# A paced row gather: 105 of 128 gathers on the GpSimd queue each wait for a point of TensorE's work

## The reference

```python
x = x + tanh(g_xattn[0]) * _L0_xattn_ref(_layernorm(x), ctx, ctx, ...)   # 16 heads, window of 32
x = x + tanh(g_ffn[0])   * _L0_ffn_ref(_layernorm(x), ...)               # 64 experts, 8 per token, and a shared one
x = x + tanh(g_xattn[1]) * _L1_xattn_ref(_layernorm(x), ctx, ctx, ...)   # 16 heads
x = x + tanh(g_ffn[1])   * _L1_ffn_ref(_layernorm(x), ...)               # 8 experts, 2 per token
```

## Time and profile before

| | us |
|---|---|
| median of three runs | 1473.32 (1467.35 to 1481.7) |
| the profiled execution | 1459.74 |
| its span, first to last instruction | 1457.9 |
| PE busy, share of the span | 1101.0, 76% |
| POOL busy, share of the span | 694.7, 48% |
| gathers L1846 into the first half's buffers: 128, mean 961 ns | 123.0 |

### The profile page before, as it was taken

The page is one execution under the profiler, slowest core; times in us unless marked ns, Lnnn a source line. Parts: engine busy times, 40 slices in busy tenths (PEclk is TensorE's granted clock), DMA queues, the critical chain, the costliest instruction groups (busy, mean ns, idle before and its releaser), DMA issues.

```text
span 1457.9 us, 28552 instructions
## 1 busy us (share of the span) xinstructions
PE 1101.0 (76%) x9014; PEld 939.3 (64%) x9014; DVE 754.7 (52%) x2773; ACT 608.3 (42%) x1505; POOL 694.7 (48%) x767
## 2 busy tenths in 40 slices
PE   4887877775778779955676771688889986789992
PEld 3666665554567768955676671467677765779992
DVE  5586666654556557724343440555666653334363
ACT  3665444432223335523333331454544452546561
POOL 1135555556556650052443437465555466554542
PEclk9998887767879889977888885576755575779996
DMA  7434114211126556643454443222311212222423
GB/s 192 92 101 122 47 50 127 70 36 45 60 91 181 165 172 190 174 118 102 135 139 120 134 135 89 67 82 70 78 48 46 58 38 66 58 61 77 133 76 108
DMA packets 228052, 144.06 MB, mean 99 GB/s; under 512 B 55058, under 2 KB 213186, under 8 KB 227906
## 3 DMA queue, kind: packets, MB, share of 16 engines
q1 hardware_dynamic: 146722, 63.14, 16.3%
q0 software_dynamic: 20992, 43.30, 9.7%
q10 hardware_dynamic: 60192, 35.79, 8.6%
HBM read 78.76 MB, written 64.49 MB: 98 GB/s over the span
## 4 chain that ended last, share of the span: by engine, by line
PE 51%; another core or an unknown queue 17%; DVE 10%; issue 10%; ACT 7%; DMA 2%; POOL 1%; SPq 1%; ACTq 1%; DVEq 0%; POOLq 0%
PE bank L846 7%; PE bank L655 5%; PE bank L642 5%; PE bank L921 4%; PE bank L931 4%; PE bank L872 3%; PE bank L616 3%; PE bank L692 3%; PE bank L823 3%; PE bank L671 2%; DVE x L1742 2%; PE bank L857 2%; PE bank L631 2%; PE bank L726 1%
## 5 line engine op out<-in xcount | busy, mean ns | idle before, releaser
L1827 POOL DMA_INDIRECT expert_rows<-xn2T,slot x256 | 252.1, 985 | 164.2 <-issue 66.4
L846 PE MATMUL bank<-wexp,arena 128*128 x768 | 154.9, 350 | 60.8 <-ACT arena L1104 42.8
L1846 POOL DMA_INDIRECT xn2T<-expert_results,slot x128 | 123.0, 961 | 153.7 <-DMA expert_results<-arena 80.7
L846 PEld LDWEIGHTS bank<-wexp,arena 128*128 128x128 f32 x768 | 127.9, 208 | 70.4 <-issue 69.2
L1611 DVE TENSOR_TENSOR arena<-arena,bank 128x176 f32<-128x176 f32 x224 | 70.7, 334 | 197.3 <-ACT arena L1109 131.9
L872 PE MATMUL bank<-wexp,arena 88*128 x768 | 112.3, 293 | 50.2 <-issue 29.3
L1109 ACT ACTIVATE arena<-bank 128x176 f32<-128x176 f32 x224 | 67.7, 317 | 171.9 <-issue 59.6
L872 PEld LDWEIGHTS bank<-wexp,arena 88*128 88x128 f32 x768 | 102.2, 207 | 55.6 <-issue 55.5
L1003 ACT ACTIVATE work<-bank 128x512 f32<-128x512 f32 x128 | 76.5, 598 | 144.2 <-PE bank L642 113.7
L1868 POOL TENSOR_SCALAR ve<-mv 128x2 f32<-128x2 f32 (+2 forms) x53 | 12.1, 228 | 243.5 <-DVE mv L1720 103.5
L655 PEld LDWEIGHTS bank<-vm,work 128*64 128x64 f32 x2048 | 94.2, 177 | 45.6 <-ACT work L1003 28.6
(11 more groups left out here) (211 smaller groups left out, 2315.2 us busy)
## 6 DMA issues: line engine op xcount, KB each, us to landing
arena<-expert_rows SPq DMA_DIRECT2D x384, 64.0 KB
expert_results<-arena ACTq DMA_DIRECT2D x96, 256.0 KB
arena<-in_ctxT ACTq DMA_DIRECT2D x32, 256.0 KB
expert_rows<-zero SPq DMA_DIRECT2D x96, 64.0 KB
xg<-expert_rows SPq DMA_DIRECT2D x80, 68.0 KB
expert_rows<-xn2T,slot POOLq DMA_INDIRECT x320
wx<-in_mix SPq DMA_DIRECT2D x16, 256.0 KB
late_rows<-expert_results SPq DMA_DIRECT2D x8, 512.0 KB
```

What stands on the lines that cost most here:

```text
L846: mm = pe.matmul(out[:, b * 2 * I0:(b + 1) * 2 * I0], xgT[:, n % 2, 2 * h + b, :], wflat[:, bass.ds(offsets[m][2 * h + b], 2 * I0)], start ...
L1827: pool.indirect_dma_start(xs, bass.IndirectOffsetOnAxis(ap=slot[:, t, k:k + 1], axis=0), xn2all[:, t, :].bitcast(I32), None).then_inc(s_sc ...
L1846: pool.indirect_dma_start(rows[:, k, :].bitcast(I32), None, ys, bass.IndirectOffsetOnAxis(ap=slot[:, t, k:k + 1], axis=0)).then_inc(ready, 16)
```

## The change

Gather i of the first half (h = 0) gets one more wait. With q = 51·5 + 2i + i // 16, it waits for signal q % 5 of PE's step n = 16 + q // 5. The five events of a step are, in order, the first and the second half of `gate_up(n+1)`, `turn_rows(n+2)`, `turn_hidden(n)` and `down(n-1)`. From step 110 on (q at or above 470) there is no wait. So gathers 0 to 104 are paced, two for every five signals with one more signal skipped per 16 gathers (5 / 2.0625 = 2.42 gathers a step), and gathers 105 to 127 are not. All other waits stay.

```diff
+GATHERS_AT = 51
...
+            def block_point(q):
+                n, event = SHB + q // 5, q % 5
+                if n + 2 < NBT:
+                    pool.wait_ge(*((b_gu, 2 * n + 3), (b_gu, 2 * n + 4), (b_xt, n + 3), (b_ht, n + 1), (b_y, n))[event])
+
...
                 elif k == 0 and t - HTILES >= LATE_RING - 4:
                     pool.wait_ge(s_comb, (t - LATE_RING + 1) * TOPK0)
+                if h == 0:
+                    block_point(GATHERS_AT * 5 + 2 * i + i // 16)
                 rows, ready, _ = gathered(t)
```

## The result

The changed kernel takes 1399.97 us, the median of four runs (1393.57 to 1404.38). The kernel before, run beside it, takes 1472.64. The ratio is 0.9494, with a 95% interval of 0.9447 to 0.9541: 73 us less.

The account below looks back on a forecast made before the run. Unbroken runs of gathers were taken to hold up plain transfers and so stop PE. Pacing would save 40 us in the stage and 4 in the tail, 44 in all, taking the median from 1473.3 to 1430 us (range 1409 to 1463).

Parts of the forecast that it names:

- The start: First mixture's second half: gather 0 waits for step 67's first signal, so the stage starts where it did, near 628 us.
- a run can't grow: Paced gathers: when PE stops, its signals and so POOL stop and plain transfers go on; no run above about six.
- The price of a paced gather: Beside the 43 steps: 0.57 us per gather, taken from the paced scatters; stage 197 us instead of 237, 40 us less.
- the tail: Behind the last gate_up: 23 unpaced gathers left instead of 26, 4 us less; next layer's first copy some 29 us behind.
- The lower bound: Plain transfers stand still only while POOL works, 0.96 us per gather: 4.23 us a step, stage 182 us, 55 us less.
- The clock: PE's granted clock over the 43 steps: expected at 0.85 or more, where it was 0.80.
- The rival of the low clock: Many small stops keep PE from 2.4 GHz: steps of 5.96 us, stage 19 us longer, 1489 us; chance 0.08.
- Late rows: DVE's additions waiting for rows of paced gathers: put at nothing, with margins of 1.6 steps and more for tiles 2 to 10.
- the half gain: Late rows for DVE or a nearly unbroken pace take 22 of the 44 us: 1452 us; chance 0.14.
- a gather costs what it costs: The 0.98 us belong to each gather, not to the run: stage 240 us, time 1473 us; chance 0.10.
- The rule of turns: Skill's rule that DMA engines alternate between queues by packet; the prediction set it aside, since breaking runs would bring nothing.

Follow-up runs that it names:

- e1: Changed kernel with all gathers waiting on signals long past, the last 23 included: 1459.32 us against 1457.45 of the kernel before, ratio 1.0009.
- e5: Changed kernel with the scatters of the stage before also laid over all five signals, 2.42 a step instead of three: 1373.47 us, ratio 0.9304.
- e4: Changed kernel with three gathers in every step instead of 2.42, until the ring holds them: 1425.27 us, ratio 0.9788.
- e12: Changed kernel plus 32 unbroken indirect gathers of evenly rising rows beside PE's steps 48 to 66: 1135.32 us, beside 1134.55 of the kernel before.
- e8: Changed kernel with the whole pacing two steps later (GATHERS_AT 53 instead of 51): 1411.02 us, ratio 0.9558.
- e3: Changed kernel at the same mean pace, but eight gathers share one point, so they come in runs of eight: 1451.71 us, ratio 0.9935.
- e15: The changed kernel itself, measured and profiled once more: 1388.56 us against 1465.86 of the kernel before, ratio 0.9478.
- e7: Changed kernel with gathers 105 to 127 also paced, by signals of the last experts and the next layer's attention: 1396.57 us, ratio 0.9458.
- e14: Same kernel as e12, run once more in another job: 1426.94 us, beside 1465.86 of the kernel before.
- e10: Changed kernel plus 32 plain 64 KB transfers started by POOL in the stage of the scatters, from step 48: 1417.18 us, beside 1477.71 of before.
- e16: Changed kernel plus 16 indirect gathers of evenly rising rows from step 48, each waiting until the last has landed: 1387.3 us, beside 1453.82 of before.
- e17: Changed kernel plus 32 indirect gathers of evenly rising rows from step 48, at most two under way: 1134.86 us, beside 1133.0 of before.
- e18: Changed kernel plus 32 indirect gathers of evenly rising rows in groups of four, each group waiting for the last's landing: 1134.88 us, beside 1133.0 of before.
- e9: Changed kernel plus 96 scratch-tile fills on POOL beside PE's steps 48 to 66: 1398.08 us, beside 1477.71 of the kernel before.

## Why the prediction was right in its direction and wrong in its size

**The start, and that a run can't grow: right.** The stage starts at 628.42, and PE's signals release the gathers. The longest run is six at the start, and twos to fours after that. Without anything to wait for (e1) the gain is zero, and the runs of four and eight give it back in part.

**The price of a paced gather: wrong, and this is the step that failed.** The forecast took 0.57 us from the paced scatters, "same pacing, same steps, same size of transfer". It measures 0.27, and (0.57 - 0.27) x 105 = 31 us. (The whole miss is 30 us: 31 in this term, 8 the other way in the tail and 1 at the start, and 7 more because the profiled execution of before lies 13.6 us under its median and that of after only 6.4.) Two of the three samenesses fail.

The pacing wasn't the same: three scatters a step is more than POOL can issue in a free step, 2.42 is less, and between the two lies the difference between a standing run and pauses of 1.2 us. e5 shows it on the scatters themselves (0.57 to 0.38), e4 on the gathers (0.43 at three a step). The prediction had both numbers, 3.05 us of POOL for a step of 3.19, and used them for the pace but not for the price.

The steps weren't the same either, so that the 3.19 that was taken off was too little. In the jobs where indirect transfers cost nothing the 16 steps of the earlier trace rows take 59.8 to 61.9 us (in e12 gate_up(27) starts at 364.57 and gate_up(43) at 424.37), 3.7 to 3.9 each, with 46 to 48 scatters and the same stores of zeros beside them. Over that, a scatter of the kernel before costs (78.5 - 59.8) / 48 = 0.39 us at most and 0.35 at least. This takes it that those steps would be as long in the slower jobs but for the effect, as PE's own pace is (3.17 and 3.19).

**The lower bound was none.** Its form, 1.91 us of plain transfers that stand still while POOL works for 2.42 x 0.96 us, gives 4.23 us a step, and the step takes 3.85. It fitted the scatter stage (4.8 for 4.91) by accident, the more so as those steps take 3.7 to 3.9 us where the scatters cost nothing. Beside single gathers the plain transfers go on: the DMA engines' share is 0.65 and the core moves 178 GB/s at POOL's 103.43 us of work. A mechanism read from the inside of long runs was carried over to runs of three, where it doesn't hold. Since the range's low end was built on it, 1400 fell outside.

**The clock: better than put.** 0.98 was measured where 0.85 or more was expected. Ahead of a gate_up of the stage PE idles for 3.03 us at most, where it was up to 9.46. Only two gate_ups run below full clock (2.71 us at 645.10 and 1.88 at 722.40). What this still costs is in the 0.27. The rival of the low clock is refuted.

**Late rows: right to put at nothing.** Of DVE's 84 additions in the stage the idle time is 1.5 us in all, and two steps later (e8) costs nothing. With it the half gain falls, and so does "a gather costs what it costs" by e1 to e3.

**The tail: not to be told.** The forecast took 4 us off because 23 gathers are left instead of 26. In this profile it is 4.4 us more, in that of e15 6.0 us less (587.2 for 593.2), so neither sign is shown. The rows behind the last gate_up, from the timeline of all engines:

```profile
819.41 0.29 DVE L1233 TENSOR_TENSOR row_f<-bank,brow 128x128 f32<-128x128 f32 x1 [19.24 <-remote]
819.82 3.26 DVE L1743 SCALAR_TENSOR_TENSOR x<-xn2T,wk,x 128x128 f32<-128x128 f32 x8
819.89 2.07 PE L693 MATMUL bank<-wv,arena 128*128 128x128 f32 x8 [11.30 <-issue]
...
823.35 0.94 POOL L1854 DMA_INDIRECT xn2T<-expert_results,slot  x1 [6.07 <-DVE x L1743]
...
846.70 1.43 DVE L1259 TENSOR_REDUCE nmax<-bank 128x8 fp32r<-128x512 f32 x2 [12.20 <-remote]
...
847.45 0.80 PE L632 MATMUL bank<-nmax,idr 128*128 128x512 f32 x1 [15.22 <-DVE nmax L1259]
...
857.29 0.87 ACT L989 ACTIVATE vm<-bank,cst 128x256 f32<-128x256 f32 x2 [30.17 <-remote]
```

Now two unbroken runs stand here. Beside the first (793.70 to 817.3) DVE waits for 19.24 us, so that tile 11 is added late and the ring holds POOL for 6.07 us. Then 24 gathers follow from 823.35 to 854.1, and in them ACT waits 30.17 us for its second copy, whose matmul (PE's L693 at 830.16) was done at 832.2. The first copy of the next layer came at 822.00, 27.9 us behind the last gate_up, as forecast (29). But it isn't where the tail is decided. That pacing this tail too brings nothing (e7) says that the gathers cost about as much wherever they lie in that layer's start.

**The rule of turns.** The Trainium skill's page "DMA: Bandwidth & Descriptors", section "Queues, rings and completion order", has DMA engines take turns between queues, packet by packet. By it the pace would have brought nothing. The trace of e14's run (a share of 0.28, 78 GB/s, a step of 35 us) doesn't agree with it for indirect gathers; that of e10 does for plain transfers from POOL (0.92, 269 GB/s, PE hardly held).

**What stays open.** Which mechanism delays the others while indirect transfers run unbroken: their waits end with a release that the profile doesn't know, also where the matmul waited for was long done. Whether a backlog of such transfers or POOL's unbroken issuing sets it: e16 changes both, and e17 and e18 fell where nothing can be seen. Whether the pace needs PE's signals or only the wider spacing. And why the kernel before takes 1133 to 1135 us in two of the seven jobs of experiments and 1454 to 1478 in the others; one of those two ran on a chip with the same number as two of the others, so it need not be the chip. In those two the gathers cost the steps nothing that shows, so the ratios of this study hold for the slower case alone; the changed kernel was never timed alone in the other, but with 32 gathers more (e12) it takes 0.8 us more than the kernel before, so the change brings little or nothing there. The stage of this study is only part of the difference between the two kinds of job: behind the last gate_up e12 takes 490.9 us and the changed kernel 597.6.

## What to carry to other kernels

Indirect transfers from GpSimd are cheap one at a time and dear in an unbroken run. Where other engines wait for plain transfers beside them, hang each on a signal of the bottleneck engine's own progress, and leave POOL slack: at a demand of 95% of a free step it was 0.27 us each, at 120% 0.43, in eights 0.84, in long runs 0.98. When a price is taken from another stage, the demand per step has to be compared as well as the kind of work, what else runs beside those steps has to be taken off first, and a bound has to come from a row that bounds it, not from a form that fits one row.

## What the runs showed of the hardware

- 32 indirect gathers of 64 KB in one run, 1.25 us apart, stop a stage that needs only plain transfers: one step of 35.0 us instead of 3.1 (e14), whether their rows are scattered or in order. 32 plain transfers of 64 KB from the same engine in 17.23 us add about 2 us (e10), and beside 96 fills of POOL the steps stay at 3.1 us (e9).
- 16 indirect gathers that each wait for the last one's landing come about 3.5 us apart and cost under 0.1 us each (e16).
- The same kernel before takes 1454 to 1478 us in some jobs and 1133 to 1135 in others; in the latter indirect gathers cost the steps nothing (e12: 3.17 us a step beside all 105 paced gathers).
